# Value products of a flash-style attention loop issued two key tiles at a time, in place of four

## The reference, cut to what matters

```python
scores = jnp.einsum('bhid,bhjd->bhij', q, k) / scale
scores = scores + _alibi_bias(N_HEADS, seq_len, M_SLOPE, x.dtype)[None]
attn = jax.nn.softmax(scores, axis=-1)
out = jnp.einsum('bhij,bhjd->bhid', attn, v)
...
x = _layernorm(x + _L0_attn_ref(x, ...), axis=-1)
x = _layernorm(x + _L0_ffn_ref(x, ...), axis=-1)
```

## Time and profile before

| | |
|---|---|
| median of three runs | 598.14 us (596.93 to 600.79) |
| the profiled execution, its own time | 600.86 us |
| its span in the trace | 598.4 us |
| mean TensorE clock granted in the span | 0.945 of full speed |
| PE busy | 530.7 us, 89% of the span |
| DVE busy | 406.8 us, 68% |
| ACT busy | 339.9 us, 57% |
| POOL (GpSimd) busy | 217.9 us, 36% |

### The profile page before, as it was taken

One profiled execution on the slowest core, in us unless ns is written; L12 is line 12 of the kernel. 1 busy time (PEld: TensorE's weight loads), 2 busy tenths in 40 slices (PEclk: granted clock), 3 DMA queues, 4 the chain that ended last, 5 costly groups with the idle time before them and its releaser, 6 DMA issues.

```text
span 598.4 us, 11849 instructions
## 1 busy us (share of the span) xinstructions
PE 530.7 (89%) x4499; PEld 298.6 (50%) x4499; DVE 406.8 (68%) x699; ACT 339.9 (57%) x665; POOL 217.9 (36%) x404
## 2 busy tenths in 40 slices
PE   6579999999999999999999999899999389999910
PEld 4234444444445454543445555555656247888710
DVE  2597877878797758789875769988695862232217
ACT  4245766767676767766777667667776013232405
POOL 5736452311234315102640520254012753554540
PEclk9797999999999999999999999999999569999965
DMA  7622343322322222221213333110000114353124
GB/s 162 172 83 76 70 122 87 96 90 77 114 87 73 91 77 100 86 82 48 69 52 70 82 87 104 29 42 21 28 12 19 58 43 109 103 142 81 54 90 133
DMA packets 49991, 48.22 MB, mean 81 GB/s; under 512 B 13923, under 2 KB 39381, under 8 KB 49936
## 3 DMA queue, kind: packets, MB, share of 16 engines
q1 hardware_dynamic: 41600, 32.26, 19.7%
q0 software_dynamic: 5488, 12.73, 6.9%
q10 hardware_dynamic: 2848, 2.49, 1.3%
HBM read 32.00 MB, written 16.06 MB: 80 GB/s over the span
## 4 chain that ended last, share of the span: by engine, by line
PE 72%; DVE 15%; DMA 5%; POOL 3%; issue 2%; ACT 1%; another core or an unknown queue 1%; POOLq 0%; ACTq 0%; DVEq 0%; SPq 0%
PE ps L958 33%; PE ps L1020 17%; DVE row_max L1486 8%; PE ps L1205 6%; PE ps L1219 5%; PE ps L960 4%; POOL xd L845 2%; DMA max_dram<-max_turned 2%; PE ps L1060 1%; DVE x_tok L1796 1%; DMA k_stacks<-k_late 1%; DVE heads L1557 1%; DMA q_stacks<-max_dram 1%; DMA w_nat<-in_qkv_w 1%
## 5 line engine op out<-in xcount | busy, mean ns | idle before, releaser
L1486 DVE TENSOR_REDUCE row_max<-ps 128x1 f32<-128x1024 f32 x256 | 297.1, 1211 | 90.6 <-PE ps L958 47.5
L1323 ACT ACTIVATE probs<-ps 128x512 f32<-128x512 f32 x512 | 268.3, 606 | 89.5 <-PE ps L960 47.8
L958 PE MATMUL ps<-k_stacks,q_stacks 96*128 96x512 bf16 x448 | 145.5, 390 | 13.7 <-DMA k_stacks<-k_late 6.1
L958 PE MATMUL ps<-q_stacks,k_stacks 99*128 99x512 bf16 (+1 forms) x512 | 142.4, 355 | 0.9 <-ACT probs L1323 0.5
L1020 PE MATMUL ps<-probs,v_unit 128*32 128x256 f32 x2048 | 124.0, 382 | 0.0
L960 PE MATMUL ps<-distance,slope_eye 128*128 128x128 bf16 x512 | 110.7, 222 | 0.0
L1020 PEld LDWEIGHTS ps<-probs,v_unit 128*32 128x32 f32 x2048 | 59.9, 109 | 51.4 <-issue 9.4
L958 PEld LDWEIGHTS ps<-k_stacks,q_stacks 96*128 96x128 bf16 x448 | 39.5, 99 | 82.8 <-DVE row_max L1486 27.9
L958 PEld LDWEIGHTS ps<-q_stacks,k_stacks 99*128 99x128 bf16 x512 | 48.7, 98 | 41.6 <-ACT probs L1323 12.2
L960 PEld LDWEIGHTS ps<-distance,slope_eye 128*128 128x128 bf16 x512 | 50.6, 99 | 26.1 <-issue 2.2
L683 POOL TENSOR_TENSOR max_parts<-row_max,no_bits 128x8 bf16<-128x8 f32 x32 | 6.5, 202 | 131.3 <-DVE row_max L1486 129.3
(11 more groups left out here) (264 smaller groups left out, 458.0 us busy)
## 6 DMA issues: line engine op xcount, KB each, us to landing
k_stacks<-k_dram SPq DMA_DIRECT2D x46, 144.0 KB
q_stacks<-q_dram SPq DMA_DIRECT2D x46, 72.0 KB
w<-in_w SPq DMA_DIRECT2D x12, 256.0 KB
xd<-blank POOLq DMA_DIRECT2D x8, 325.0 KB, 2.7
probs<-xd SPq DMA_DIRECT2D x8, 325.0 KB
k_stacks<-in_c_alibi_k SPq DMA_DIRECT2D x24, 96.0 KB
out_dram<-out_t SPq DMA_DIRECT2D x16, 128.0 KB
yt<-zeros POOLq DMA_DIRECT2D x4, 512.0 KB, 3.0
```

The lines of the kernel that those rows point to most:

```text
L958: mm = pe.matmul(out, lhs, rhs, start=True, stop=at is None)
L1323: act.activation(probs[:, k % KEPT, HALF * e:HALF * (e + 1)], ps[:, ring_of(n), :], ACT.Exp).then_inc(ring_read, 1)
L1486: dve.tensor_reduce(row_max[:, m % 2, i:i + 1], max_pair(k).rearrange("p a n -> p (a n)"), AX.X, ALU.max).then_inc(mx_used, 1)
```

## The change

`values` now takes a pair of key tiles. Behind every second row (rows 1, 3, 5 and 7) it issues the pair that lies two pairs behind the one just scored (`BEHIND = 2`). So the key tiles 2 and 3 of the group before still follow the fourth row of a group, and key tiles 0 and 1 come two rows earlier than before. Place 2 stays behind the fourth row. Place 3 moves between the two key tiles of the pair that follows it; before, two key tiles stood on each side. Behind the last row three pairs are left, where there were four. The names `TAIL_FIRST` and its slices go; it was empty.

```diff
+BEHIND = 2
...
-            def values(m, group, half):
-
-                for j in range(GROUP * group, GROUP * (group + 1)):
-                    if j % GROUP == 2:
-                        for stage, c in (hooks(half, (3,)) if half < HALVES else TAIL_FIRST):
+            def values(pair, half, places):
+
+                m = pair // (NB // 2)
+                for j in range(2 * pair % NB, 2 * pair % NB + 2):
+                    if j % 2 == 1:
+                        for stage, c in hooks(half, places):
                             late(stage, c)
                     if j == 0:
                         pe.wait_ge(v_copied, min(m, FOURS + SLOTS - 1) + 1)
...
-                    for stage, c in hooks(half, (2,)):
-                        late(stage, c)
-                    if group == 1:
-                        values(m, 0, half)
-                    elif m > 0:
-                        values(m - 1, 1, half)
-            values(UNITS - 1, 1, HALVES)
+                        if j % GROUP == GROUP - 1:
+                            for stage, c in hooks(half, (2,)):
+                                late(stage, c)
+                        pair = (NB * m + j) // 2 - BEHIND
+                        if j % 2 == 1 and pair >= 0:
+                            values(pair, half, (3,) if j % GROUP == GROUP - 1 else ())
+            for pair in range(NB * UNITS // 2 - BEHIND, NB * UNITS // 2):
+                values(pair, HALVES, ())
```

More of the change, by code:

```diff
@@ L96 @@
 )
-TAIL_FIRST = ()
-TAIL = TAIL_FIRST + ((ATT_T, 3), (ROUTE_A, 2), (PROJECT2, 3), (ROUTE_B, 2), (EXP_LOGITS, 2), (RANK, 2), (HID2, 3), (STATS2, 3),
+TAIL = ((ATT_T, 3), (ROUTE_A, 2), (PROJECT2, 3), (ROUTE_B, 2), (EXP_LOGITS, 2), (RANK, 2), (HID2, 3), (STATS2, 3),
                      (ROOT2, 3), (T2, 3), (SLOT, 2), (SCATTER0, 2), (LOGITS, 3), (RECIP_A, 4), (TURN, 4), (SCATTER1, 2),
@@ L1168, in _ @@
             pe.wait_ge(o_kept, PAIRS)
-            for stage, c in TAIL[len(TAIL_FIRST):]:
+            for stage, c in TAIL:
                 if (stage, c) == (RANK, LAST):
```

## The result

The changed kernel takes 608.99 us (median of four runs, 608.49 to 610.10) against 597.53 for the kernel before: a ratio of 1.0179, interval 1.0141 to 1.0217, so 11.5 us or 1.8% slower. Its profiled execution took 608.49 us with a span of 606.6.

The account below looks back on a forecast made before the run. PE's order of issue was taken to set the time. 12.4 - 8.6 - 0.8 + 1.8 + 0.8 + 3.5 = +9.1 us on the profiled 600.86 gave 610.0, on the median 607.2 us; range 597.5 to 613.

Parts of the forecast that it names:

- Edges: In 59 halves with value products, entry and exit of one added stretch cost 0.21 each: +12.4 us.
- Late rows: In 27 halves without the diagonal, the late third and fourth rows vanish, 0.32 a half: -8.6 us.
- waits for a reduction under 10: Sign in the changed profile: the count of waits for a reduction should fall from 60 to under 10.
- Long waits: At four long waits for a reduction, the added edges disappear, 0.21 each: -0.8 us.
- `RANK`: At bands 0 and 1, two key tiles stand ahead instead of four, so PE waits 0.87 longer each: +1.8 us.
- The late DMA: At one row 0, the late arrival of row maxima by DMA loses cover: +0.8 us.
- The copy: In even units, value products behind row 5 wait 0.38 or 0.20 for ACT's copy of ps_o: +3.5 us.
- Units 30 and 31: Unit 30's copy wait, up to 1.3, against 0.9 less behind the last row: taken as 0, 1 either way.

Follow-up runs that it names:

- e3: The kernel before, stretches of four key tiles kept, each cut in its middle by one bf16 matmul over the whole array adding zero to ps_o; 614.15 us, 1.0271.
- e4: The kernel after with ACT's copy of ps_o issued ahead of row 4's exponentials, and one key tile behind every row; 636.29 us, 1.0635.
- e2: The kernel after with RANK of bands 0 and 1 moved from place 0 to place 1, behind two rows and a stretch; 608.21 us, 1.0178.
- e1: The kernel after with ACT's copy of ps_o issued ahead of row 4's exponentials in place of behind them; 606.41 us, 1.0153.
- e8: The kernel after with stretches of four restored in units 30 and 31 alone; 611.13 us, 1.0170.
- e7: The kernel before with RANK of bands 0 and 1 moved to place 1, stretches of four kept; 598.88 us, 0.9972.
- e5: The kernel before with pairs only in groups whose exponentials hold no diagonal, not in the last two units, and the early copy of e1; 607.29 us, 1.0103.
- e6: e5 with RANK of bands 0 and 1 moved to place 1; 606.51 us, 1.0102.

## Why the prediction was right, point by point

The forecast was 607.2 us with +9.1 on the profiled execution. Measured are 609.0, and 11.5 between the medians. Over the halves 1 to 59 without 7 and 8 the two traces differ by 380.38 - 370.79 = 9.6 us; the forecast for these was 8.3 (9.1 less the 0.8 of the DMA). The mechanism was right, with one term mis-sized and two wrong. The number came out closer than the terms did: the edges and unit 30 cost 6 us more than forecast, and less than that shows in the medians, so part of the closeness is luck.

- **Edges, +12.4.** Right in kind, low in size: 0.24 and not 0.21 a stretch, by e3, e4 and the halves, so 14.2. The mis-sized part is the exit, 0.14 for 0.12. The rule of the Trainium skill, TensorEngine Tiling (Array Packing), Key Properties, that a change of the tiling mode drains the array, fits the sign; read as a wait for the whole recorded 0.38 of a matmul it would give 0.32, and e3 excludes that. What the 0.24 consists of inside the engine stays open.
- **Late rows, -8.6.** They are gone; a half without the diagonal lost 0.09 net, which with edges of 0.24 is 0.33 for them, 8.9 in 27 halves. The check that the prediction offered (waits for a reduction under 10) was a wrong reading of that row, not of the mechanism.
- **Long waits, -0.8.** Right: units 18 and 26 did not grow (7.66 for 7.74, 7.53 for 7.53). The other two of the four waits stand in the two halves ahead of `RANK`, so these swallow their added edge as well.
- **`RANK`, +1.8.** Right: these two halves are 0.82 and 0.87 longer, with nothing for the edge, the waits grew from 0.49 to 1.39 and from 0.60 to 1.46, and e2 takes them away.
- **The late DMA, +0.8.** Not borne out. In the profiled executions of all eleven kernels the halves 7 and 8 take between 12.7 and 18.3 us, with no order by kernel. So it is taken for chance. How much of the scatter of the medians comes from it is not shown, for only one execution of each kernel is profiled.
- **The copy, +3.5.** Right: in most units 0.41 to 0.42 without the diagonal and 0.23 to 0.24 with it, 3.6 in sum by e1. Units 12, 18 and 28 pay less (0.14, 0.24 and 0.20), and unit 20, which was put at nothing, pays 0.20.
- **Units 30 and 31, 0 with 1 either way.** This was the term that failed. They cost 4.3 us in the halves 60 to 62, and 0.5 more from the first score of half 63 to the end of the loop's value products. The prediction saw "a wait of up to 1.3" and set against it the pair fewer behind the last row. The wait was 1.66, and the granted clock fell to its lower level until 455 us, which the prediction had nowhere. e1 and e8 show that both come from the wait for the copy: with it shortened to 0.68 (e1) or gone (e8) the half takes 7.29 or 6.56 in place of 9.85, and the clock stays at its upper level.

The terms as measured, 14.2 - 8.9 - 0.9 + 1.7 + 3.6 = 9.7 for the halves 1 to 59, and 4.3 behind them, make 14.0, and half 63 adds 0.5. The medians differ by 11.5. The spans of the two profiled executions differ by 606.6 - 598.4 = 8.2, and there every part can be named: +9.6 (halves 1 to 59 without 7 and 8), +4.3 (halves 60 to 62) and +0.5 (half 63), then -0.7 (halves 7 and 8), -3.7 (all that lies ahead of half 1) and -1.8 (all behind the loop). The last three follow no edit. The first score of unit 1 comes at 59.1 us in the kernel before, but at 58.5 in e7 and 56.8 in e3, which keep its order there, and the earliest is at 55.1; what lies behind the loop takes between 134.7 and 137.9; and halves 7 and 8 differ by up to 5.6. The kernel before happened to be profiled in a long execution, 600.86 with a median of 597.53. Between the medians these parts can't be told apart.

## What to carry to other kernels

In this kernel a stretch of work in another tiling of the array has a price of entry and exit; count the stretches before they are split, and set the price against the stalls that splitting removes. Here that was 0.24 against 0.33 in one kind of half and against nothing in the other. When a burst is split and half of it is moved ahead, list each wait that stood behind the burst and each wait of the burst itself: the first lose cover, the second come earlier, and both together were the larger part of this loss (1.7, 3.6 and 4.3, where edges less late rows make 5.3). An idle spell that is short for the sum can still cost twice, because the granted clock may be lower behind it, as behind the 1.66 us in unit 30.

## What the runs showed that had not been expected

The granted clock behind a wait of PE is not given by the wait's length. In e1 PE waited 3.0 us for the row maxima ahead of unit 4 and went on at the upper level. In e5, at the same place, it waited only 1.9 us, but the granted clock was 0.50 from 96 to 98 us, and the next half took 7.81 in place of 6.16. In e6 it waited 3.1 us and went on at the lower level for some 6 us, and the next half took 8.73. First e1, then e6, the wait and the clock of the stretches behind it:

```profile
94.57 0.39 PE L958 MATMUL ps<-k_stacks,q_stacks 96*128 96x512 bf16 x1 [2.95 <-DMA q_stacks<-max_dram]
```

```profile
94.50:96.50 2.00, 1.93 (x13) 1.09 (x14) 1.23 (x2) 0.95 (x2) 0.00 (x0) 1.00 0.28 66
```

```profile
95.33 0.61 PE L958 MATMUL ps<-k_stacks,q_stacks 96*128 96x512 bf16 x1 [3.12 <-DMA q_stacks<-max_dram]
```

```profile
95.00:97.00 2.00, 1.67 (x6) 0.80 (x7) 0.49 (x1) 0.00 (x0) 0.00 (x0) 0.50 0.34 75
97.00:99.00 2.00, 2.00 (x9) 0.92 (x7) 1.20 (x2) 1.13 (x2) 0.00 (x0) 0.50 0.26 84
99.00:101.00 2.00, 2.00 (x9) 0.92 (x7) 1.20 (x2) 1.13 (x2) 0.00 (x0) 0.50 0.20 73
```

Why the row maxima come so late in this one place, from nothing (e4) to 3.1 us beyond what covers them, was not tried. Two loads of experts' weights are issued shortly before (at 89.5 and 90.1 us in the kernel before), and whether they have to do with it is not shown.
